# ScalarE's sixteen attention iterations: a loop against written-out code

## The reference

```
xn = layernorm(x)                                # x: 4 batches x 2048 x 256, fp32
q, k, v = xn @ Wq.T, xn @ Wk.T, xn @ Wv.T        # 16 heads of 16
q, k = rope(q), rope(k)
scores = einsum(q, k) / sqrt(16); causal mask
out = softmax(scores) @ v @ Wo.T
gate, up = fp4_linear(xn, w_gate), fp4_linear(xn, w_up)      # 256 -> 704, blocks of 16 quantised
out of kernel = x + out + fp4_linear(silu(gate) * up, w_down)
```

## Time and profile before

| | us |
|---|---|
| median of 3 runs | 2635.87 |
| the runs | 2633.4 to 2637.86 |
| the profiled execution | 2636.0 |
| its span, first to last instruction | 2634.1 |
| mean granted TensorE clock | 0.967 |
| attention stage in the trace, about | 851 to 2546 |

### The profile page before, as it was taken

How to read it: one execution, slowest core, us unless ns; L and a number is a source line. 1 busy time by engine, 2 the same in 40 slices (tenths; PEclk the granted TensorE clock), 3 DMA queues, 4 the chain that set the end, 5 groups by cost and what they waited for, 6 DMA issues and landing times. The chain is left out here.

```text
span 2634.1 us, 53516 instructions
## 1 busy us (share of the span) xinstructions
PE 2455.1 (93%) x14338; PEld 1176.5 (45%) x14338; DVE 2245.0 (85%) x4836; ACT 1606.0 (61%) x3261; POOL 85.9 (3%) x271
## 2 busy tenths in 40 slices
PE   4799999999997899999999999999999999999778
PEld 2455556556554244444444344344343343333236
DVE  8898898898897998898898898889888888888515
ACT  2445454554453277777777777777777777777530
POOL 0000000000000000000000000000000000000100
PEclk8899999999999599999999999999999999999889
DMA  5111121121122512212112112122112112110114
GB/s 186 56 65 59 67 72 57 63 72 59 60 72 69 129 34 61 67 33 65 57 43 65 39 58 69 31 63 66 35 60 65 40 54 71 34 48 10 67 63 175
DMA packets 141387, 168.37 MB, mean 64 GB/s; under 512 B 14049, under 2 KB 107537, under 8 KB 141201
## 3 DMA queue, kind: packets, MB, share of 16 engines
q1 hardware_dynamic: 137856, 159.49, 19.3%
q10 hardware_dynamic: 3344, 6.41, 0.7%
HBM read 97.17 MB, written 67.90 MB: 63 GB/s over the span
## 5 line engine op out<-in xcount | busy, mean ns | idle before, releaser
L1182 ACT ACTIVATE prob<-score 128x512 f32<-128x512 f32 (+3 forms) x2560 | 1153.0, 546 | 452.4 <-PE score L1118 235.2
L1257 DVE TENSOR_REDUCE top<-tile 128x1 f32<-128x512 f32 x1536 | 957.5, 681 | 103.9 <-PE tile L1088 96.3
L1113 PE MATMUL score<-qs,ks 99*128 99x512 bf16 (+3 forms) x2560 | 815.3, 351 | 39.0 <-DMA qs<-row 17.0
L1088 PE MATMUL tile<-ks,qs 96*128 96x512 bf16 (+3 forms) x2560 | 776.5, 355 | 24.3 <-DMA ks<-qkp 15.7
L1133 PE MATMUL acc<-prob,vs 128*32 128x512 f32 (+3 forms) x5120 | 535.2, 536 | 0.0
L1262 DVE CUSTOM_DVE_ANT_0 tile<-tile,mask 128x128 f32<-128x128 f32 (+3 forms) x1024 | 469.9, 519 | 74.1 <-PE tile L1088 71.8
L1113 PEld LDWEIGHTS score<-qs,ks 99*128 99x128 bf16 x2560 | 244.6, 97 | 454.0 <-ACT prob L1182 248.4
L1088 PEld LDWEIGHTS tile<-ks,qs 96*128 96x128 bf16 x2560 | 238.8, 98 | 292.2 <-DVE top L1257 81.8
L335 PE MATMUL gu<-wguT,xT 128*128 128x512 f32 (+1 forms) x768 | 313.5, 561 | 16.2 <-DVE hid L678 16.2
L1133 PEld LDWEIGHTS acc<-prob,vs 128*32 128x32 f32 x5120 | 133.8, 109 | 245.0 <-issue 135.5
L335 PEld LDWEIGHTS gu<-wguT,xT 128*128 128x128 f32 x768 | 144.7, 192 | 162.7 <-issue 124.2
(11 more groups left out here) (114 smaller groups left out, 1624.7 us busy)
## 6 DMA issues: line engine op xcount, KB each, us to landing
qkp<-parts SPq DMA_DIRECT2D x192, 128.0 KB
vscr<-vt SPq DMA_DIRECT2D x16, 1024.0 KB, 4.5
vs<-vscr SPq DMA_DIRECT2D x16, 1024.0 KB, 5.9
oscr<-acc_sb SPq DMA_DIRECT2D x64, 256.0 KB, 2.1
qs<-qkp SPq DMA_DIRECT2D x64, 192.0 KB, 3.4
ks<-qkp SPq DMA_DIRECT2D x64, 192.0 KB, 3.4
x_all<-in_x SPq DMA_DIRECT2D x16, 512.0 KB, 9.0
qs<-qkp SPq DMA_DIRECT2D x64, 128.0 KB, 3.1
```

What stands on the lines that cost most here:

```text
L1088: mm = nc.tensor.matmul(bank[:, h * width:(h + 1) * width], qs[par][0:ROWS, h0 + h, q0:q0 + P], ks[par][0:ROWS, h0 + h, k0:k0 + width], st ...
L1113: mm = nc.tensor.matmul(bank[:, 0:width], ks[par][0:ROWS_M, h, kb * P:(kb + 1) * P], qs[par][0:ROWS_M, h, qb * GROUP + off:(qb + 1) * GROU ...
L1182: nc.scalar.activation(prob[:, k % PROB_SLOTS, 0:width], score[:, k % SCORE_SLOTS, 0:width], ACT.Exp, scale=HEAD ** -0.5).then_inc(probs_r ...
L1257: nc.vector.tensor_reduce(top[:, j, h0, c:c + 1], bank, AX.X, ALU.max).then_inc(tile_taken, 1)
```

## The change

ScalarE's loop over the attention iterations becomes a Python loop: the same body is written sixteen times, one behind the other. In the two functions `iteration` calls, the iteration number is then a plain number instead of a register.

```
             def iteration(it):
                 for e in plan:
                     if e[0] == "scores":
                         exponentials(it, e)
                     elif e[0] == "weigh" and e[1] == last_step[e[2]]:
                         take_acc(it, e)
 
-            with loop(nc, act, ITERS) as it:
+            for it in range(ITERS):
                 iteration(it)
```

## The result

| | median us | ratio to before, 95% interval |
|---|---|---|
| before, 4 runs | 2636.86 | |
| changed kernel, 4 runs | 2619.40 | 0.9936 [0.9921, 0.9951] |
| the same again, 5 runs beside 15 of before (2636.03) | 2621.77 | 0.9944 [0.9931, 0.9958] |

The account below looks back on a forecast made before the run. It took three engines tied by short rings, all stalling for one table load per iteration, as the bound; 9 x 1.21 + 2.33 = 13.2 us off 2636.0, less 0.1 for the median, gave 2622.7, range 2613 to 2629.5.

Parts of the forecast that it names:

- What bounds: Attention stage: TensorE, ScalarE and VectorE tied by rings of three score and four tile banks, all stalling for one load.
- Branch and register work at 0: ScalarE's loop branch, hint and register instructions lie beside the copy or under exponentials; removing them was taken as 0.
- Eight of the nine boundaries at 1.21: Iteration ends without a TensorE or VectorE back edge: each gains VectorE's whole idle gap, 1.21 us; nine were counted.
- Six boundaries at 0.44 and less: Iteration ends where TensorE and VectorE branch back: only VectorE's remaining gaps, 0.38 to 0.51 us, come back; 2.33 us together.
- The boundary that I counted as 0: The sixth boundary with a VectorE back edge: no load gap was shown in the timeline, so 0 gain.
- The fifteenth iteration: First iteration written out behind VectorE's loop, with its 2.12 us "issue" stall; the boundary ahead was counted at 1.21 us.
- the sum: Gains over all boundaries between attention iterations: 9 x 1.21 + 2.33 = 13.2 us.
- The load that stays at 0: The one remaining load, behind the first score, delays the first exponential by 1.28 us but costs 0; without cover 1.28 once.
- Code fetch as the slower rival: ScalarE's straight instruction stream stalls for code like VectorE's: 4 to 16 us slower, about 2646; chance 0.08.
- More by a page's figure: Loads between iterations at 2.66 us each, fifteen times: 40 us, 2596; the rival of more than 21.2 us had chance 0.08.

Follow-up runs that it names:

- e2: Changed kernel with a table load put back at each of the fifteen boundaries between attention iterations; 2636.30 us, ratio 1.0000 to before.
- e8: Changed kernel with a table load ahead of the twelfth exponential of each iteration but the first, where ScalarE idles anyway; 2620.93 us, ratio 0.9944.
- e1: Kernel before, ScalarE's loop kept, with a one-column exponential ahead of it, so the loop's body has no table load; 2620.74 us, ratio 0.9942.
- e9: Kernel before with a one-column exponential ahead of ScalarE's kept loop and only VectorE's loop written out; 2610.62 us, ratio 0.9907.
- e6: Changed kernel with VectorE's loop written out as well; 2610.93 us, ratio 0.9905 to before.
- e3: Changed kernel with a one-column exponential ahead of the attention iterations, so the one load runs early; 2621.11 us, ratio 0.9940.
- e4: Changed kernel with table loads put back only at the nine boundaries without a back edge of TensorE and VectorE; 2632.65 us, ratio 0.9989.
- e5: Changed kernel with table loads put back only at the six boundaries where TensorE and VectorE branch back; 2623.38 us, ratio 0.9957.
- e7: Changed kernel with the loops of VectorE, TensorE and SP written out as well; 2609.57 us, ratio 0.9905 to before.

## Why the prediction was right, and where it was not

- **What bounds.** Right: three engines tied by short rings, all standing for one load. e2 against e8 is the proof that the place decides.
- **Branch and register work at 0.** Right within 0.06 us a boundary (e1), and e9.
- **Eight of the nine boundaries at 1.21** (the ninth is the one ahead of the fifteenth iteration, below). Too low for six, and about right for two only because something else took time there. The kind without a back edge gave 100.69 - 99.28 = 1.41, ScalarE's full share and not VectorE's gap. The step that was mis-sized is to take VectorE's idle time for its stop. Its 512-wide instructions last 0.68 to 0.69 us and follow each other every 0.60, so an idle time of 1.21 costs 1.21 + 0.08 = 1.29 from start to start: the masked tile came 3.84 behind the copy and comes 2.55 behind it now. The remaining 0.12 came further on. VectorE gained 0.04 in the next reductions, and 16.75 us behind the copy it waited 0.20 us for TensorE, a gap that I had not put among the rows. The same place before and after:

```profile
1023.16 5.47 DVE L1257 TENSOR_REDUCE top<-tile 128x1 f32<-128x512 f32 x9 [0.20 <-PE tile L1088]
```

```profile
1019.39 5.47 DVE L1257 TENSOR_REDUCE top<-tile 128x1 f32<-128x512 f32 x9
```

  Now it comes 15.35 behind the copy, 1.4 sooner, and VectorE still idles there, for 0.1 us; a timeline row does not print so short an idle time, the groups of 1019.3 to 1020 do:

```profile
L1257 DVE TENSOR_REDUCE top<-tile 128x1 f32<-128x512 f32 x2 | 1.3, 686 | 0.1
```

  So VectorE has slack there before and after, and what TensorE and ScalarE got back, the full 1.41, goes through. Two of these iterations, 99.56 long, gave 1.13 and 1.14 (a delay of 0.27 late in the iteration, see code fetch); the eight boundaries together gave 10.8 where 8 x 1.21 = 9.7 was counted.
- **Six boundaries at 0.44 and less.** The mechanism was right and the size too small: 0.58 to 0.65 at five of them and 0.32 at one, together 3.4 for 2.3. The 0.08 was missing here too: at the second boundary the masked tile gained 3.84 - 3.28 = 0.56 for an idle time of 0.44. The earlier trace rows is the place up to which it holds, and the wait of 0.18 for VectorE at 1107.41 shows who limits. The rest is VectorE's own stop at its back edge, which I took for constant and which is not. The boundary that I counted as 0 had a long one in the kernel before (first row); the one that gave only 0.32 has a long one in the changed kernel (second row):

```profile
1914.47 1.88 DVE L1257 TENSOR_REDUCE top<-tile 128x1 f32<-128x512 f32 x3 [1.05 <-PE tile L1088]
```

```profile
1304.45 1.89 DVE L1257 TENSOR_REDUCE top<-tile 128x1 f32<-128x512 f32 x3 [0.95 <-PE tile L1088]
```

  At the other boundaries of this kind the stop is 0.66 to 0.79 before and 0.65 to 0.70 after. e6, which takes VectorE's back edge away, brings these iterations to 99.6 to 99.8.
- **The fifteenth iteration.** Here the sum failed in its result, but not by its boundary. I counted 1.21 for the boundary ahead of it; the iteration took 104.56 where it had taken 104.33. VectorE's stall for "issue", which I used as a rival's evidence, was still there and 2.28 instead of 2.12 us. What it sets off is longer than itself. The windows of the changed kernel behind the stall:

```profile
2347.00:2351.00 4.00, 1.57 (x9) 0.51 (x8) 1.72 (x11) 2.03 (x5) 0.27 (x1) 0.88 0.02 4
2351.00:2353.00 2.00, 2.00 (x9) 0.57 (x11) 1.91 (x8) 1.13 (x2) 0.00 (x0) 0.50 0.00 0
2353.00:2355.00 2.00, 2.00 (x16) 0.40 (x8) 0.00 (x0) 0.00 (x0) 0.00 (x0) 0.50 0.00 0
2355.00:2357.00 2.00, 2.00 (x10) 0.66 (x7) 0.04 (x1) 0.52 (x1) 0.00 (x0) 0.53 0.00 0
```

  TensorE idles 2.43 us for VectorE, and then its granted clock is 0.50, the 1.2 GHz level, for about 7 us. In the kernel before, TensorE idled 2.27 us and its clock was back at 1.00 within 4 us:

```profile
2366.00:2368.00 2.00, 1.11 (x4) 0.53 (x5) 2.00 (x11) 0.04 (x1) 0.00 (x0) 0.64 0.01 4
2368.00:2370.00 2.00, 2.00 (x10) 0.40 (x12) 1.14 (x6) 1.09 (x2) 0.00 (x0) 0.51 0.00 0
2370.00:2372.00 2.00, 2.00 (x20) 0.75 (x13) 0.19 (x1) 0.51 (x2) 0.00 (x0) 1.00 0.00 0
```

  The same iteration in e3 (no load ahead of it) and in e4 (with a load):

```profile
2302.88:2406.14 103.26, 100.74 (x709) 40.19 (x708) 89.74 (x233) 74.55 (x164) 4.03 (x16) 0.98 0.09 30
```

```profile
2312.15:2415.14 102.99, 99.56 (x709) 39.86 (x708) 89.90 (x233) 76.00 (x166) 4.05 (x16) 1.00 0.10 30
```

  The clock orders the lengths. Without a load ahead of the iteration it takes 104.48 to 104.68 at a mean clock of 0.97 (the changed kernel twice, and e1) and 103.26 to 103.29 at 0.98 (e3, e5, e8); with a load 104.33 and 104.56 at 0.98 (before, e2) and 102.99 at 1.00 (e4). So at the same clock of 0.98 the load costs 1.0 to 1.3 us there, near the 1.21 that was counted, and the longer time at the low level took 1.2 to 1.4 back. The sum had no term for that. How long the clock stays low is not settled by the stall: with the same 2.43 us of idle TensorE it was about 7 us in the changed kernel and about 3 in e3, and with the same 2.27 it was about 3 in the kernel before and nothing in e4. What decides it is open.
- **The last boundary** gave 115.78 - 114.34 = 1.44 us at the same clock of 0.91, which fits the full share. But it is one pair, and the last iteration also takes 116.5 to 116.6 without a load when its clock is 0.90 (e3, e5).
- **The load that stays at 0.** Right: the fourth score comes 2.85 us behind the first, with the load early or late (e3).
- **Code fetch as the slower rival.** It did not come: no "issue" wait of ScalarE in the attention stage of the changed kernel, and e7 has none on VectorE or TensorE in it. What straight code may cost is small: the written-out kernels have one or two iterations that are 0.1 to 0.3 us longer than their like (the two of 99.56 here), e2, e4, e5 and e8 show one or two "issue" waits of ScalarE of 0.2 to 0.3 us, and e1 and e9, with the loop, have neither. The cause was not tried. Its premise that VectorE's stall is a rate of straight code was wrong: written out from the start, VectorE has none (e6), so the stall goes with the loop that was left. That it is a fetch of code is not shown. The Trainium skill ("Runtime: NRT & Kernel Launch", Instruction fetch mechanics) has the sequencer stream straight code by itself, the crossing of a block mostly hidden. e6 and e7 agree: VectorE's "issue" waits in the attention stage are gone, and in e7 TensorE's too.
- **More by a page's figure.** "ScalarE: Activation LUTs" of the Trainium skill (What ACT_TABLE_LOAD costs) has 2.66 us for a load and its drain at a switch to a different set. The estimate of 40 us took that figure for loads that switch nothing: between two of them ScalarE does only exponentials and copies, and e1 gives the same gain with a single one. Such a load cost 1.41 on ScalarE (1.89 against 0.48 from copy to exponential), and the runs exclude the 40 us.
- **The ranges.** The prediction gives its forecast as 2615 to 2626 in the sum and as 2615 to 2627 with the chances; both medians lie in either.
- **Terms that cancelled.** The eight boundaries gave 1.1 us more than counted, the six 1.0 more, and the fifteenth iteration 1.4 less; the sum, 13.2 for 13.9, looks better than its terms, and that is luck: the 1.4 is a longer time at the low clock, which another profile need not have had.

## What to carry to other kernels

Look at what a compiler puts into a loop's body: a table load there is paid in each turn, and one tiny instruction ahead of the loop that needs the table takes it out (e1), with no code written out. Price a stall by where it stands: in a gap of its engine fifteen loads cost nothing, at a boundary at which the other engines' rings run full they cost 15.7 us (e2 against e8), although the engine is busy only 75% of the time. The gain of a removed stall is the stalled engine's own share, if each tied engine can give back as much: the stop that the stall made on it, counted from start to start and not by the idle time alone, plus its slack up to where the engines meet next. Compare iterations at the same granted clock before their difference is put down to an edit.

## What the runs showed of the hardware that was not expected

- A stall of VectorE of 2.1 to 2.4 us for "issue" in the written-out iterations behind a loop that it left, once in each of the nine profiles with VectorE's loop; gone when the loop was written out as well (e6), with 5.2 us for its whole effect.
- TensorE's granted clock falls to 0.50 after it idled 2.3 to 2.6 us for that stall, and stays there for about 3 or about 7 us; in one profile of the nine (e4, 2.27 us idle) it stayed at 1.00. The idle times of 1.03 us at the boundaries left it at 1.00.
- At each second boundary VectorE's branch back comes with an idle time of 0.65 to 1.05 us, which varies from one time to the next and is 0.08 when VectorE's loop is written out (e6), although the profile puts it down to TensorE's tile. TensorE's branch back shows as 0.2 to 0.3 us and ScalarE's as 0.06, in the same program and with the same hint.
